# Relation counts of an adjacency layer: one-hots of the relations as weights instead of one-hots of the destinations

## The chip, the cores and the metric

The kernel runs on one core of a Trainium2 chip. The metric is the device time of one execution in microseconds, the median of three runs. The engines are TensorE (PE in the profile, its weight loads PEld), VectorE (DVE), ScalarE (ACT), GpSimd (POOL) and SyncE (SP), which issues most of the DMAs.

## What is computed

Four graph layers run one after the other on 3125 nodes of 128 features and 53125 edges (25000 drawn ones, their reverse, and a loop for each node), each followed by an addition of its input and a layer normalisation. Layer 0 is an attention layer, layer 1 sums the neighbours' rows, layer 2 weights them by an edge network, and layer 3 is a relational one:

```
rel_vec = rel_emb[edge_type]                        # 64 relations
msg = (x[src] + rel_vec) @ W_msg.T + b_msg
agg = segment_sum(msg, dst) / max(deg, 1)
out = x @ W_self.T + b_self + agg
```

Layer 3's sum of relation vectors into a node is the node's count of edges per relation times the table of 64 vectors. Neither those counts nor the adjacency matrix depends on features, and layer 1 needs the adjacency matrix as well. So both are built once, in layer 1.

## The kernel before, in words

Nodes are padded to 25 blocks of 128 (NB = 25). Edges are sorted into slots: a tile of 128 slots for each pair of a destination block and a source block. The phases follow one another: placing of the edges and the edge network (to some 200 us), layer 0 with gathers and scatters as one-hot matmuls (to 509 us), the **adjacency layer**, layer 1 (509 to 682 us), then layer 2 (gathers and scatters again) and layer 3, which reads the stored adjacency back.

The adjacency layer runs over 7 banks q of destination blocks (`even(q)`: four blocks in banks 0 to 3, three in banks 4 to 6) and, in each, over 25 source blocks b. That is 175 steps s = 25 q + b, and `even_width(q)` is 512 or 384 columns. For each step:

- VectorE makes the one-hots of the step's slots (`set_hots`, L1950) in one tile of `ring` (`ohs`, six buffers): for each slot the source node (128 values) and the relation (64 values). The block index d lies innermost, so that block d's one-hot has a stride of 4 elements. `ohx` holds the same for an extra tile of each bank, which is used at b = 0 and on the diagonal.
- The destination one-hots were stored in layer 0 (`hots_d`). SyncE loads them (L774, L778), contiguous for each block, into parts of `big` and `XT`, in chunks of five steps, four chunks ahead.
- TensorE's `build(s)` runs for each block d of the bank a matmul of the source one-hot (weights) with the destination one-hot (moving, 128 columns) into a bank that four steps take in turn (L2581; L2584 for the extra tile): the 128 x 128 block of the adjacency matrix. Then, for each block, it runs the relation counts (L2588; L2591 for the extra tile): **destination one-hot as weights, relation one-hot moving, 64 columns**. They add up over the whole bank q in PSUM bank 5 + q % 2, which a matmul with zeros clears first (L2560).
- ScalarE copies the adjacency block to fp32r (L1286); it or VectorE copies it to bytes (L1289, L1965), which SyncE stores for layer 3 (L804).
- TensorE's `apply1(s)` multiplies it by the features: two matmuls of 512 or 384 columns (L2611), adding up in PSUM bank 3 + q % 2; after a bank's last step the bank's own features are added (L2618), and VectorE copies the sums to `AG` (`sums_out1`, L1959, five steps into the next bank; `ag_ready`).

TensorE's program is written out by hand: two builds, then two applications, the builds two steps ahead. VectorE, ScalarE and SyncE keep to the same order of steps.

The counts of bank q stand in PSUM as destination x relation, while layer 3 needs relation x destination. So after bank q's last step ScalarE copies them to SBUF (`crelT`, L1295; semaphore `crelT_cp`). After the application of step 7 of bank q + 1 (after the last bank: at once), TensorE turns them (`rel_turned`, L2598), which needs `ag_ready`, since the transposes go to the bank of the sums (3 + q % 2). At b = 9 of bank q + 1 ScalarE copies the turned counts to `crel` (`rel_rows`, L1276; `crel_cp`) and SyncE stores them (L793).

At the end stands `dense` (L2642), the layer's weight matmul on seven groups of four blocks. Group i writes PSUM bank i, and VectorE adds each to the input (`relu_add`, L1994). Statistics, normalisation (ScalarE, L1227) and transposes follow in series.

Of the kernel before, what the change touches and what calls it, by code (L numbers as in the profile page):

```python
# [13 lines left out]
P = 128  # L14
# [14 lines left out]
NREL = 64  # L29
# [18 lines left out]
def gnn_kernel(nc, ins, out):  # L48
# [161 lines left out]
    with ctx:  # L210
# [3 lines left out]
        def sem(name):  # L214
            return ctx.enter_context(nc.semaphore(name))
# [80 lines left out]
        adjf = adjf_r[:, :].rearrange("p (r n) -> p r n", r=XBUF)  # L296
        identr = identr_r[:, :]
        crel = ring[:, 10240:10240 + 4 * 4 * P].bitcast(fp32).rearrange("p (r n) -> p r n", r=2)
        crelT = XT[:, HC:HC + 2 * CT].rearrange("p (r n) -> p r n", r=2)
        adj3 = ring[:, 0:3 * ACH * 2 * P].bitcast(u8).rearrange("p (r n) -> p r n", r=3)  # L300
        crel3 = ring[:, 7680:7680 + 4 * 4 * P].bitcast(fp32).rearrange("p (r n) -> p r n", r=2)

# [140 lines left out]
        def bank(i):  # L443
            return PS[:, 512 * i:512 * (i + 1)]
# [100 lines left out]
        applied = sem("applied")  # L545
        acc = sem("acc")
        crel_cp = sem("crel_cp")
        crel_tr = sem("crel_tr")
        crelT_cp = sem("crelT_cp")
        crel_io = [sem(f"crel_io{n}") for n in range(2)]  # L550
        ag_ready = sem("ag_ready")
        post = sem("post")
# [473 lines left out]
        def _(act):  # L1026
# [243 lines left out]

            def rel_rows(q):
                w = even_width(q)
                act.wait_ge(crel_tr, q + 1)
                if q >= 2:
                    act.wait_ge(crel_io[q % 2], 16 * (q // 2))
                C.copy(crel[0:NREL, q % 2, 0:w], bank(3 + q % 2)[0:NREL, 0:w]).then_inc(crel_cp, 1)  # L1276

            for q in range(BANKS):
                w = even_width(q)
                for b in range(NB):  # L1280
                    s = q * NB + b
                    act.wait_ge(adj_mm, s + 1)
                    if s >= XBUF:
                        act.wait_ge(applied, s - XBUF + 1)
                        dve_copied(act, s - XBUF)
                    C.copy(adjf[:, s % XBUF, 0:w], adj_bank(s)[:, 0:w]).then_inc(adjf_cp, 1)  # L1286
                    if not by_dve(s):
                        adj_free(act, s)
                        C.copy(adj_slot(s), adj_bank(s)[:, 0:w]).then_inc(adj_act, 1)  # L1289
                    if q == 0 and b % 2 == 0 and HBANK - 1 + b // 2 < BANKS:  # L1290
                        round_rows(1, HBANK - 1 + b // 2)
                    if q and b == 9:
                        rel_rows(q - 1)
                act.wait_ge(rel_mm, (q + 1) * NB)
                C.copy(crelT[:, q % 2, 0:w // 2], bank(5 + q % 2)[:, 0:w // 2]).then_inc(crelT_cp, 1)  # L1295
            rel_rows(BANKS - 1)

            normalise(2, X)
# [988 lines left out]
        def _(pe):  # L2287
# [234 lines left out]
            def sums(L):  # L2522
                kind, K, past = min(L, 1), gen_own(L), gen_past(L)
                if L == 1:
                    pe.wait_ge(ag_ready, BANKS)
                    pe.wait_ge(crelT_cp, BANKS)
                    pe.wait_ge(rc_cp, 1)
                    for b in range(NB):
                        o = T.transpose(PS[:, b * P:(b + 1) * P], X[:, b, :], ident[:, :])
                    o.then_inc(g_own, 1)  # L2530
                with pe.Fori(0, NCH) as c, pe.Fori(0, NB) as w:
                    m = pe.snap(c * (K + 2 * NB) + w * 2)
                    pe.wait_ge(g_step[kind], m + (past + K + 3))
                    if L == 0:
                        T.matmul(bank(0)[:, 0:VW], g_oh, g_vals, start=True, stop=True).then_inc(g_mm[kind], 1)
                    else:
                        T.matmul(bank(0)[:, 0:P], g_vals[:, 0:F], g_oh, start=True, stop=True).then_inc(g_mm[kind], 1)
                pe.wait_ge(g_step[kind], past + gen_total(L))
# [15 lines left out]
            def build(s):  # L2554
                q, b = s // NB, s % NB
                if b == 0:
                    pe.wait_ge(ohs_ready, q * JN + 2)
                    if q >= 2:
                        pe.wait_ge(crelT_cp, q - 1)
                    T.matmul(bank(5 + q % 2)[:, 0:even_width(q) // 2], zeros[0:1, 0:P], zeros[0:1, 0:even_width(q) // 2],  # L2560
                             start=True, stop=False, skip_group_check=True)
                pe.wait_ge(ohs_ready, q * JN + b + 2)
                if s == 3:
                    pe.wait_ge(rc_cp, 1)
                if s >= 4:
                    pe.wait_ge(adjf_cp, s - 3)
                    act_copied(pe, s - 4)
                c = q * NCK + b // ACH
                if b % ACH == 0:
                    hots_wait(pe, c)  # L2570
                both = even(q)

                def hots(buf, to, d):
                    return (buf[:, 0:OH1].rearrange("p (n b) -> p n b", b=4)[:, :, d], to[:, d, :],
                            buf[:, OH1:OH1 + CT].rearrange("p (n b) -> p n b", b=4)[:, :, d])

                usual = (ohs[:, s % SBUF, :], hots_in[c % HBUF][:, :, b % ACH, :])
                extra = (ohx[:, q % 2, :], hots_ex[:, q % 2, :, :])
                for d, blk in enumerate(both):
                    s1, d1, _ = hots(*usual, d)  # L2580
                    o = T.matmul(adj_bank(s)[:, d * P:(d + 1) * P], s1, d1, start=True, stop=blk != b)  # L2581
                    if blk == b:
                        s1, d1, _ = hots(*extra, d)
                        o = T.matmul(adj_bank(s)[:, d * P:(d + 1) * P], s1, d1, start=False, stop=True)  # L2584
                o.then_inc(adj_mm, 1)
                for d, blk in enumerate(both):
                    _, d1, r1 = hots(*usual, d)
                    o = T.matmul(bank(5 + q % 2)[:, d * NREL:(d + 1) * NREL], d1, r1, start=False, stop=False, skip_group_check=True)  # L2588
                    if b == 0:
                        _, d1, r1 = hots(*extra, d)  # L2590
                        o = T.matmul(bank(5 + q % 2)[:, d * NREL:(d + 1) * NREL], d1, r1, start=False, stop=False, skip_group_check=True)  # L2591
                o.then_inc(rel_mm, 1)

            def rel_turned(q):
                pe.wait_ge(crelT_cp, q + 1)
                pe.wait_ge(ag_ready, q + 1)
                for d in range(len(even(q))):
                    o = T.transpose(bank(3 + q % 2)[0:NREL, d * P:(d + 1) * P], crelT[:, q % 2, d * NREL:(d + 1) * NREL], ident[:, :])  # L2598
                o.then_inc(crel_tr, 1)

            def apply1(s):
                q, b = s // NB, s % NB
                w = even_width(q)
                if b == 0 and q >= 2:
                    pe.wait_ge(crel_cp, q - 1)
                if q == 0:
                    pe.wait_ge(xp_rest, b // 4 + 1)
                pe.wait_ge(adjf_cp, s + 1)
                to = bank(3 + q % 2)
                for part, xs in enumerate((XH, XL)):  # L2610
                    o = T.matmul(to[:, 0:w], xs[:, b, :], adjf[:, s % XBUF, 0:w], start=b == 0 and part == 0, stop=False, skip_group_check=True)  # L2611
                o.then_inc(applied, 1)
                if b == NB - 1:
                    if q == 0:
                        pe.wait_ge(identr_ready, 1)
                    for d, blk in enumerate(even(q)):
                        for xs in (XH, XL):
                            o = T.matmul(to[:, d * P:(d + 1) * P], xs[:, blk, :], identr, start=False, stop=False, skip_group_check=True)  # L2618
                    o.then_inc(acc, 1)
# [4 lines left out]
            for s in range(0, NS, 2):  # L2624
                for n in (s + 2, s + 3):
                    if n < NS:
                        build(n)
                for n in (s, s + 1):
                    if n < NS:
                        apply1(n)  # L2630
                        if n >= NB and n % NB == 7:
                            rel_turned(n // NB - 1)
            rel_turned(BANKS - 1)
            with pe.If(general == 1):
                sums(1)

# [16 lines left out]

            def sums1_wait(i):
                pe.wait_ge(ag_ready, (even_need(i) if i < 3 else BANKS))
                if i == 3:
                    pe.wait_ge(crel_cp, BANKS)
                if i >= 5:
                    pe.wait_ge(crelT_cp, BANKS)
                if i == 0:  # L2660
                    pe.wait_ge(rc_cp, 1)

            dense(post, sums1_wait, [(AG, W1[:, :])])
# [182 lines left out]
```

## Time and profile before

| | |
|---|---|
| median of 3 runs | 1089.4 us (1089.07 to 1090.24) |
| profiled execution | 1089.84 us, its span 1088.0 us |
| TensorE busy | 1002.6 us, 92% |
| VectorE busy | 861.1 us, 79% |
| ScalarE busy | 691.3 us, 64% |
| granted TensorE clock, mean | 0.971 |
| adjacency layer | 509 to 682 us of the span |

The profile is that of one execution. A line such as `L2588 PE MATMUL PS<-ring,big 128*128 128x64 bf16` is a group of instructions of one source line: engine, operation, tiles written and read, weights (partitions * columns) and moving operand (partitions x columns). A matmul's duration holds its latency, so several are in flight at a time; the distance of their starts is what the engine spends on one. In a timeline, neighbours of one line are merged into one row ("x4"), which gives the first start and the time to the last end.

### The profile page before, as it was taken

What the parts mean: (1) busy time and instruction counts of PE and PEld (TensorE: products, weight loads), DVE (VectorE), ACT (ScalarE), POOL (GpSimd) and SP (SyncE); (2) the same over time, 40 slices, a digit from 0 to 9 for tenths busy, and PEclk for the clock granted to TensorE, in tenths of its full rate; (3) what the DMA queues carried; (4) which work ended last, traced back from release to release, by engine and by line L of the source; (5) the groups of instructions that cost most, each with busy time, mean ns of one, the idle gap of its engine ahead of it and who ended that gap; (6) DMA issues with size and microseconds to landing.
All of it is one profiled execution on the core that took longest, in us unless ns stands there. A gap on an engine that the chain in (4) does not pass through costs nothing.

```text
span 1088.0 us, 27899 instructions
## 1 busy us (share of the span) xinstructions
PE 1002.6 (92%) x10463; PEld 874.7 (80%) x10463; DVE 861.1 (79%) x1934; ACT 691.3 (64%) x1489; POOL 218.2 (20%) x260
## 2 busy tenths in 40 slices
PE   3798979699999999995999999779999999989997
PEld 3343557599999999995788889669999999976775
DVE  6875999988998989987766677788787888766754
ACT  3467765454555555456888888577677776776554
POOL 4501340000000000000000000126666666610000
PEclk9899999899999999997999999889999999999998
DMA  6000020366767677752866564235444445334232
GB/s 159 1 2 1 4 68 3 121 207 225 238 215 225 222 238 227 204 175 72 292 195 193 172 201 141 82 104 140 138 136 129 131 131 139 109 112 124 69 99 82
DMA packets 86925, 150.38 MB, mean 138 GB/s; under 512 B 14524, under 2 KB 58375, under 8 KB 86557
## 3 DMA queue, kind: packets, MB, share of 16 engines
q1 hardware_dynamic: 65609, 116.01, 35.9%
q10 hardware_dynamic: 16122, 22.16, 5.7%
q0 software_dynamic: 5056, 10.36, 3.9%
q8 instruction: 88, 1.44, 0.5%
q14 instruction: 50, 0.40, 0.1%
HBM read 112.56 MB, written 35.94 MB: 136 GB/s over the span
## 4 chain that ended last, share of the span: by engine, by line
PE 81%; DVE 10%; ACT 4%; issue 3%; DMA 2%; POOL 0%; POOLq 0%; DVEq 0%; SPq 0%; ACTq 0%
PE PS L2500 14%; PE PS L2705 14%; PE PS L2488 11%; PE PS L2688 8%; PE PS L2611 7%; PE PS L2791 6%; PE PS L2581 3%; PE PS L2588 3%; PE PS L2326 2%; PE PS L2339 2%; DVE ring L1659 2%; DVE vo L1663 2%; PE PS L2403 2%; ACT X L1227 1%; PE PS L2357 1%
## 5 line engine op out<-in xcount | busy, mean ns | idle before, releaser
L1151 ACT CAST vo<-XT 128x768 f32<-128x768 bf16 (+1 forms) x218 | 180.3, 827 | 163.7 <-PE PS L2705 64.2
L984 POOL DMA_INDIRECT XT<-tab,ring x158 | 159.9, 1012 | 113.5 <-PE PS L2705 60.2
L2500 PE MATMUL PS<-vo 128*128 128x133 f32 x1300 | 175.9, 284 | 1.2 <-ACT vo L1151 1.2
L2500 PEld LDWEIGHTS PS<-vo 128*128 128x128 f32 x1300 | 157.2, 191 | 1.4 <-issue 1.4
L2488 PE MATMUL PS<-kp,ring 128*128 128x132 bf16 x1950 | 146.7, 221 | 3.2 <-DVE ring L1631 1.7
L2705 PE MATMUL PS<-vo 128*128 128x128 f32 x984 | 132.8, 279 | 0.0
L2488 PEld LDWEIGHTS PS<-kp,ring 128*128 128x128 bf16 x1950 | 125.6, 97 | 5.4 <-DVE ring L1631 1.8
L1641 DVE TENSOR_TENSOR XT<-iotab,XT 128x768 bf16<-128x768 bf16 (+1 forms) x218 | 120.0, 551 | 3.2 <-DMA hots_d<-XT 1.5
L2705 PEld LDWEIGHTS PS<-vo 128*128 128x128 f32 x984 | 118.9, 191 | 3.0 <-issue 2.4
L2490 PE MATMUL PS<-SDP,ring 128*128 128x12 bf16 x650 | 110.2, 170 | 0.0
L1286 ACT CAST adjf_r<-PS 128x512 fp32r<-128x512 f32 (+1 forms) x175 | 92.4, 550 | 25.4 <-PE PS L2581 23.6
L1631 DVE TENSOR_SCALAR ring<-ring,pcolm 128x1664 bf16<-128x1664 bf16 x146 | 91.2, 652 | 18.9 <-PE PS L2688 15.5
L1767 DVE TENSOR_TENSOR vo<-PS,vo 128x768 f32<-128x768 f32 (+1 forms) x109 | 103.2, 947 | 0.7 <-ACT vo L1201 0.5
L2107 DVE TENSOR_TENSOR vo<-PS,EWS 128x640 f32<-128x640 f32 (+2 forms) x109 | 82.3, 755 | 27.1 <-PE PS L2688 26.9
L2688 PE MATMUL PS<-kp,ring 128*128 128x128 bf16 x1476 | 99.9, 219 | 0.8 <-ACT big L1308 0.8
L965 POOL IOTA ring<- 128x650 int32 x1 | 0.8, 759 | 477.5 <-PE PS L2588 477.5
L2688 PEld LDWEIGHTS PS<-kp,ring 128*128 128x128 bf16 x1476 | 91.3, 98 | 2.3 <-ACT big L1308 1.0
L1950 DVE TENSOR_TENSOR ring<-IN,SLc 128x768 bf16<-128x768 bf16 x182 | 91.4, 550 | 0.0
L2791 PE MATMUL PS<-adjf_r,xh_r 128*128 128x512 f32 (+1 forms) x175 | 70.6, 404 | 7.2 <-DVE adjf_r L2255 3.4
L2611 PE MATMUL PS<-adjf_r,xh_r 128*128 128x512 f32 (+1 forms) x175 | 72.9, 417 | 0.0
L1103 ACT ACTIVATE kp<-PS 128x512 f32<-128x512 f32 x104 | 57.6, 608 | 23.0 <-PE PS L2326 22.1
L2611 PE MATMUL PS<-adjf_r,xl_r 128*128 128x512 f32 (+1 forms) x175 | 65.3, 373 | 0.0
(350 smaller groups left out, 2008.6 us busy)
## 6 DMA issues: line engine op xcount, KB each, us to landing
ring<-rows_d SPq DMA_DIRECT2D x146, 416.0 KB, 5.8
hots_d<-XT ACTq DMA_DIRECT2D x108, 192.0 KB, 4.7
big<-hots_d SPq DMA_DIRECT2D x10, 640.0 KB, 5.3
XT<-hots_d SPq DMA_DIRECT2D x10, 640.0 KB, 4.8
adj_d<-ring SPq DMA_DIRECT2D x20, 320.0 KB, 2.4
big<-hots_d SPq DMA_DIRECT2D x8, 480.0 KB, 4.4
adj_d<-ring SPq DMA_DIRECT2D x15, 240.0 KB, 2.1
ring<-adj_d SPq DMA_DIRECT2D x11, 320.0 KB, 3.0
```

Of the source, the lines that this page charges most:

```text
L984: G.indirect_dma_start(far_rows[:, f % FBUF, :], None, tab[2], bass.IndirectOffsetOnAxis(ap=far_row[:, t:t + 1], axis=0)).then_inc(far_in[ ...
L1151: C.copy(ohd[:, k % 3, 0:n, :], ohb[:, k % 3, 0:n, :]).then_inc(hots_wide, 1)
L1286: C.copy(adjf[:, s % XBUF, 0:w], adj_bank(s)[:, 0:w]).then_inc(adjf_cp, 1)
L1641: V.tensor_tensor(ohb[:, k % 3, 0:n, :].rearrange("p t (h d) -> p t h d", d=2), iotab[:, :].rearrange("p (h d) -> p h d", d=2).unsqueeze(1 ...
L1767: V.tensor_tensor(va[:, :, :, 0:F].rearrange("p a i (h f) -> p a i h f", h=H), gathered(k, 0, F).rearrange("p a i (h f) -> p a i h f", h=H ...
L2488: T.matmul(PS[:, to:to + ROW0], ohT[:, 0, h % OBUF, l * P:(l + 1) * P], KP[:, source(t), part, :], start=part == 0, stop=part == 2)
L2490: T.matmul(PS[:, to + ROW0:to + ROW0 + 3 * H], ohT[:, 1, h % OBUF, l * P:(l + 1) * P], SDP[:, t // JN, :, :].rearrange("p t h -> p (t h)") ...
L2500: T.matmul(bank(6 + b % 2)[:, 0:VW], ohd[:, k % 3, i, :], vals[:, k % 3, i, :], start=j == 0, stop=j == JN - 1).then_inc(scattered, 1)
L2611: o = T.matmul(to[:, 0:w], xs[:, b, :], adjf[:, s % XBUF, 0:w], start=b == 0 and part == 0, stop=False, skip_group_check=True)
L2688: o = T.matmul(PS[:, to:to + F], ohT[:, 0, h % OBUF, l * P:(l + 1) * P], XP[:, source(t), part, :], start=part == 0, stop=part == 2)
L2705: T.matmul(bank(6 + q % 2)[:, (b % 4) * P:(b % 4 + 1) * P], rows_of(k, i, t), ohd[:, k % 3, i, :], start=j == 0, stop=j == JN - 1).then_in ...
L2791: o = T.matmul(to[:, 0:w], xs[:, b, :], adjf[:, s % XBUF, 0:w], start=b == 0 and part == 0, stop=False, skip_group_check=True)
```

## The change

The operands of the relation matmuls are exchanged: the relation one-hot (64 columns, at a stride of 4 elements) becomes the weights, the destination one-hot (128 columns, contiguous) moves. The result is relation x destination in 64 partitions and 128 columns for each block, up to a whole PSUM bank. The zeroing matmul is as wide. The transposes, `crelT`, its copies and the two semaphores go. ScalarE copies the counts straight from bank 5 + q % 2 to `crel`, at b = 2 of the next bank instead of b = 9; TensorE's waits follow: the clearing of a counts bank waits for `crel_cp` two banks back, the first application in a bank of sums for `ag_ready` two banks back, and the weight matmuls at the end wait for all ScalarE's byte copies before group 0 and for `crel_cp` only before group 5.

```diff
--- before.py
+++ after.py
@@ -296,7 +296,6 @@
         adjf = adjf_r[:, :].rearrange("p (r n) -> p r n", r=XBUF)
         identr = identr_r[:, :]
         crel = ring[:, 10240:10240 + 4 * 4 * P].bitcast(fp32).rearrange("p (r n) -> p r n", r=2)
-        crelT = XT[:, HC:HC + 2 * CT].rearrange("p (r n) -> p r n", r=2)
         adj3 = ring[:, 0:3 * ACH * 2 * P].bitcast(u8).rearrange("p (r n) -> p r n", r=3)
         crel3 = ring[:, 7680:7680 + 4 * 4 * P].bitcast(fp32).rearrange("p (r n) -> p r n", r=2)
 
@@ -545,8 +544,6 @@
         applied = sem("applied")
         acc = sem("acc")
         crel_cp = sem("crel_cp")
-        crel_tr = sem("crel_tr")
-        crelT_cp = sem("crelT_cp")
         crel_io = [sem(f"crel_io{n}") for n in range(2)]
         ag_ready = sem("ag_ready")
         post = sem("post")
@@ -1270,10 +1267,10 @@
 
             def rel_rows(q):
                 w = even_width(q)
-                act.wait_ge(crel_tr, q + 1)
+                act.wait_ge(rel_mm, (q + 1) * NB)
                 if q >= 2:
                     act.wait_ge(crel_io[q % 2], 16 * (q // 2))
-                C.copy(crel[0:NREL, q % 2, 0:w], bank(3 + q % 2)[0:NREL, 0:w]).then_inc(crel_cp, 1)
+                C.copy(crel[0:NREL, q % 2, 0:w], bank(5 + q % 2)[0:NREL, 0:w]).then_inc(crel_cp, 1)
 
             for q in range(BANKS):
                 w = even_width(q)
@@ -1289,10 +1286,8 @@
                         C.copy(adj_slot(s), adj_bank(s)[:, 0:w]).then_inc(adj_act, 1)
                     if q == 0 and b % 2 == 0 and HBANK - 1 + b // 2 < BANKS:
                         round_rows(1, HBANK - 1 + b // 2)
-                    if q and b == 9:
+                    if q and b == 2:
                         rel_rows(q - 1)
-                act.wait_ge(rel_mm, (q + 1) * NB)
-                C.copy(crelT[:, q % 2, 0:w // 2], bank(5 + q % 2)[:, 0:w // 2]).then_inc(crelT_cp, 1)
             rel_rows(BANKS - 1)
 
             normalise(2, X)
@@ -2523,7 +2518,7 @@
                 kind, K, past = min(L, 1), gen_own(L), gen_past(L)
                 if L == 1:
                     pe.wait_ge(ag_ready, BANKS)
-                    pe.wait_ge(crelT_cp, BANKS)
+                    pe.wait_ge(crel_cp, BANKS)
                     pe.wait_ge(rc_cp, 1)
                     for b in range(NB):
                         o = T.transpose(PS[:, b * P:(b + 1) * P], X[:, b, :], ident[:, :])
@@ -2556,8 +2551,8 @@
                 if b == 0:
                     pe.wait_ge(ohs_ready, q * JN + 2)
                     if q >= 2:
-                        pe.wait_ge(crelT_cp, q - 1)
-                    T.matmul(bank(5 + q % 2)[:, 0:even_width(q) // 2], zeros[0:1, 0:P], zeros[0:1, 0:even_width(q) // 2],
+                        pe.wait_ge(crel_cp, q - 1)
+                    T.matmul(bank(5 + q % 2)[0:NREL, 0:even_width(q)], zeros[0:1, 0:NREL], zeros[0:1, 0:even_width(q)],
                              start=True, stop=False, skip_group_check=True)
                 pe.wait_ge(ohs_ready, q * JN + b + 2)
                 if s == 3:
@@ -2585,24 +2580,17 @@
                 o.then_inc(adj_mm, 1)
                 for d, blk in enumerate(both):
                     _, d1, r1 = hots(*usual, d)
-                    o = T.matmul(bank(5 + q % 2)[:, d * NREL:(d + 1) * NREL], d1, r1, start=False, stop=False, skip_group_check=True)
+                    o = T.matmul(bank(5 + q % 2)[0:NREL, d * P:(d + 1) * P], r1, d1, start=False, stop=False, skip_group_check=True)
                     if b == 0:
                         _, d1, r1 = hots(*extra, d)
-                        o = T.matmul(bank(5 + q % 2)[:, d * NREL:(d + 1) * NREL], d1, r1, start=False, stop=False, skip_group_check=True)
+                        o = T.matmul(bank(5 + q % 2)[0:NREL, d * P:(d + 1) * P], r1, d1, start=False, stop=False, skip_group_check=True)
                 o.then_inc(rel_mm, 1)
-
-            def rel_turned(q):
-                pe.wait_ge(crelT_cp, q + 1)
-                pe.wait_ge(ag_ready, q + 1)
-                for d in range(len(even(q))):
-                    o = T.transpose(bank(3 + q % 2)[0:NREL, d * P:(d + 1) * P], crelT[:, q % 2, d * NREL:(d + 1) * NREL], ident[:, :])
-                o.then_inc(crel_tr, 1)
 
             def apply1(s):
                 q, b = s // NB, s % NB
                 w = even_width(q)
                 if b == 0 and q >= 2:
-                    pe.wait_ge(crel_cp, q - 1)
+                    pe.wait_ge(ag_ready, q - 1)
                 if q == 0:
                     pe.wait_ge(xp_rest, b // 4 + 1)
                 pe.wait_ge(adjf_cp, s + 1)
@@ -2628,9 +2616,6 @@
                 for n in (s, s + 1):
                     if n < NS:
                         apply1(n)
-                        if n >= NB and n % NB == 7:
-                            rel_turned(n // NB - 1)
-            rel_turned(BANKS - 1)
             with pe.If(general == 1):
                 sums(1)
 
@@ -2653,11 +2638,10 @@
 
             def sums1_wait(i):
                 pe.wait_ge(ag_ready, (even_need(i) if i < 3 else BANKS))
-                if i == 3:
+                if i == 5:
                     pe.wait_ge(crel_cp, BANKS)
-                if i >= 5:
-                    pe.wait_ge(crelT_cp, BANKS)
                 if i == 0:
+                    act_copied(pe, NS - 1)
                     pe.wait_ge(rc_cp, 1)
 
             dense(post, sums1_wait, [(AG, W1[:, :])])
```

## Rows read from the trace of the kernel before

**Rows 1.** The page, busy time and share of the span of TensorE.

```profile
PE 1002.6 (92%) x10463; PEld 874.7 (80%) x10463; DVE 861.1 (79%) x1934; ACT 691.3 (64%) x1489; POOL 218.2 (20%) x260
```

**Rows 2.** Busy us by stretch: length, PE, PEld, DVE, ACT, POOL, clock, DMA share, GB/s.

```profile
549.00:576.00 27.00, 27.00 (x281) 22.21 (x280) 17.43 (x38) 22.14 (x44) 0.00 (x0) 1.00 0.64 197
```

**Rows 3.** Timeline of a pair of four-block steps: start us, us, engine line, tiles.

```profile
581.43 0.42 PE L2581 MATMUL PS<-big,ring 128*128 128x128 bf16 x4
...
581.69 0.40 PE L2588 MATMUL PS<-ring,big 128*128 128x64 bf16 x4
...
581.91 0.41 PE L2581 MATMUL PS<-big,ring 128*128 128x128 bf16 x4
...
582.15 0.40 PE L2588 MATMUL PS<-ring,big 128*128 128x64 bf16 x4
...
582.36 0.47 PE L2611 MATMUL PS<-adjf_r,xh_r 128*128 128x512 f32 x1
...
583.38 0.41 PE L2581 MATMUL PS<-big,ring 128*128 128x128 bf16 x4
```

**Rows 4.** Timeline early in the first bank, with the wait for a one-hot.

```profile
524.90 0.26 PEld L2581 LDWEIGHTS PS<-XT,ring 128*128 128x128 bf16 x4 [0.58 <-DVE ring L1950]
```

**Rows 5.** Timeline of TensorE, three-block steps: a plain pair, then one with transposes.

```profile
645.45 0.36 PE L2581 MATMUL PS<-XT,ring 128*128 128x128 bf16 x3
...
646.93 0.36 PE L2581 MATMUL PS<-XT,ring 128*128 128x128 bf16 x3
647.13 0.34 PE L2588 MATMUL PS<-ring,XT 128*128 128x64 bf16 x3
647.29 0.35 PE L2581 MATMUL PS<-XT,ring 128*128 128x128 bf16 x3
...
648.74 0.36 PE L2581 MATMUL PS<-XT,ring 128*128 128x128 bf16 x3
```

**Rows 6.** Timeline of the four-block pair that holds the transposes.

```profile
549.89 0.41 PE L2581 MATMUL PS<-XT,ring 128*128 128x128 bf16 x4
...
552.27 0.41 PE L2581 MATMUL PS<-XT,ring 128*128 128x128 bf16 x4
```

**Rows 7.** Timeline of the layer's end.

```profile
679.39 0.48 ACT L1289 CAST ring<-PS 128x384 uint8<-128x384 f32 x1
...
680.61 0.27 PE L2618 MATMUL PS<-identr_r,xl_r 128*128 128x128 f32 x1
680.92 0.56 DVE L1959 COPY big<-PS 128x384 f32<-128x384 f32 x1 [1.87 <-PE PS L2618]
...
682.02 5.82 PE L2642 MATMUL PS<-W,big 128*128 128x128 f32 x50
...
683.19 0.69 DVE L1994 SCALAR_TENSOR_TENSOR big<-PS,X 128x512 f32<-128x512 f32 x1 [1.71 <-PE PS L2642]
```

**Rows 8.** Single lines, ns min/median/max; the last two, of the page: busy us, mean ns.

```profile
L2581 PEld LDWEIGHTS PS<-big,ring x320: 111/115/152, 510.1 to 674.4; 128*128 128x128 bf16 x160
...
L2588 PEld LDWEIGHTS PS<-ring,big x320: 96/98/152, 510.5 to 674.6; 128*128 128x128 bf16 x160
L2588 PE MATMUL PS<-ring,big x320: 217/239/261, 510.6 to 674.6; 128*128 128x64 bf16 x160
...
L2318 PEld LDWEIGHTS PS<-identb,big x104: 123/124/209, 35.5 to 139.5; 128*99 128x99 bf16 x104
...
L2705 PEld LDWEIGHTS PS<-vo 128*128 128x128 f32 x984 | 118.9, 191 | 3.0 <-issue 2.4
...
L2688 PE MATMUL PS<-kp,ring 128*128 128x128 bf16 x1476 | 99.9, 219 | 0.8 <-ACT big L1308 0.8
```

**Rows 9.** Timelines elsewhere: plain matmuls, ones behind 99-column loads, fp32 weight loads.

```profile
819.82 0.94 PE L2688 MATMUL PS<-kp,ring 128*128 128x128 bf16 x14
...
59.86 0.39 PE L2318 MATMUL PS<-identb,big 128*99 128x128 bf16 x4
...
820.54 1.08 PEld L2705 LDWEIGHTS PS<-vo 128*128 128x128 f32 x9
```

## The prediction

> **What bounds the kernel now.** I read the page's busy shares, then a table of busy time by stretch over the adjacency layer, then the timeline of single steps there, steps with four destination blocks and with three, and last the end of the layer. TensorE is busy for 92% of the span [rows 1], so an edit in its stream may count. In the adjacency layer TensorE is busy for the whole of a stretch of 27.00 us, with ScalarE at 22.14 and VectorE at 17.43 [rows 2]. ScalarE and VectorE thus have a sixth or more to spare, and TensorE sets the pace. The timeline says the same: a pair of steps runs from 581.43 to 583.38 us, 1.95 us, and consecutive TensorE rows follow without a gap [rows 3]. Only early in the first bank does TensorE wait for one-hots; the last time is at 524.90 [rows 4], some 14 steps in, so I take 14 of the 100 four-block steps (banks 0 to 3) as covered by waits, and 86 plus the 75 three-block steps (banks 4 to 6) as TensorE bound. That is 86 x 4 + 75 x 3 = 569 relation matmuls that count.
>
> The rows start by start give the price of a matmul, since lasting 219 or 239 ns is latency and the spacing is what is paid. In the pair of rows 3 the adjacency matmuls (L2581) take 0.26 + 0.24 us for eight, 0.0625 each; the relation matmuls (L2588) take 0.22 + 0.21 us for eight, 0.054 each. In a three-block step they take 0.20 and 0.16 us for three, 0.067 and 0.053 [rows 5].
>
> **The change, part by part.**
>
> *Turns inside the layer, removed.* A pair of four-block steps that holds the four transposes runs from 549.89 to 552.27, 2.38 us [rows 6] against 1.95: 0.43. A three-block pair with its three runs from 646.93 to 648.74, 1.81 us, and the plain pair before it from 645.45, 1.48 us [rows 5]: 0.33. Turns of banks 0 to 3 and 4 to 5: 4 x 0.43 + 2 x 0.33 = **-2.4 us**.
>
> *The tail.* Today the last applications start at 680.61, VectorE copies the sums from 680.92 for 0.56 us, only then do the last transposes run, and the dense matmuls (L2642) begin at 682.02; VectorE takes their first bank at 683.19, 1.17 us later [rows 7]. After the change the first dense bank needs only the sums of bank 0, and ScalarE's last byte copy, which starts at 679.39 and lasts 0.48 us [rows 7], so it can begin at some 680.72. VectorE would take it at 681.9, after its own copy (until 681.48). **-1.3 us**. Behind it stands a serial chain (VectorE's additions and statistics, ScalarE's scaled rows), so I expect it kept. Relation bank 6 is needed only at the dense matmuls' bank 5, microseconds later; nothing waits there. Late next is VectorE's own sequence.
>
> *The zeroing matmul, wider.* It goes from 256 to 512 columns (192 to 384). At the 0.0555 us that 128 bf16 columns take [rows 9] (worked out below), 256 more columns are 0.111 us and 192 are 0.083. Six banks after the first: 3 x 0.111 + 3 x 0.083 = **+0.6 us**; the lower bound is nothing, if the wait for a one-hot covers it. In bank 0 it is covered.
>
> *The copies.* ScalarE loses seven copies of counts and keeps the other seven, moved from the tenth step of a bank to the third. With a sixth to spare these are nothing; the cover is TensorE's pace, and a copy of 0.6 us put into the wrong place costs at most a part of that, seven times. ScalarE's idle share is spread over the steps, so I take 0. SyncE's store of the counts waits for the copy, which now comes earlier, and the block loads queued behind it are four ahead: 0. TensorE's new waits (the count copy two banks back in place of the turned copy; the sums two banks back) are for things done most of a bank earlier: 0.
>
> *The relation matmul itself.* This is the open term. Before: weights 128 columns, contiguous, moving 64 columns at a stride of 4 elements. After: weights 64 columns at that stride, moving 128 contiguous. The moving side first. The 64 strided columns last 239 ns, more than the 219 ns of 128 contiguous ones, and are spaced 0.054 us, not half of a 128-column matmul [rows 3, 8]. Fourteen plain 128-column matmuls elsewhere take 0.94 us: (0.94 - 0.219) / 13 = 0.0555 each [rows 9]. So doubling the columns costs 0.0015 each, 569 x 0.0015 = +0.9. On this the Trainium skill disagrees: TensorE: Matmul & The Clock Gate, section Back-to-back issue gap, has N / 2.4 + 2.5 ns at the full clock, so about 29 ns for 64 columns and 56 for 128; SBUF — State Buffer, section Door 1 (the passage on 16-byte cachelines), lets bf16 be strided by up to 8 elements for free, so it would not excuse the strided read either. By these the edit would add 27 ns to each, some +15 us. This case's trace disagrees: 0.054 us for 64 columns; the measurement decides.
>
> Then the weight side. A 128-column strided load lasts 115 ns against 98 contiguous, and a contiguous one of 99 columns 124 ns [rows 8]: fewer columns aren't quicker, narrower loads seem to run in a slower form. Four matmuls behind such 99-column loads are still spaced (0.39 - 0.219) / 3 = 0.057 [rows 9]. Loads of 128 fp32 columns follow each other every (1.08 - 0.191) / 8 = 0.111 us [rows 8, 9], so 64 columns at that rate need 0.056. Both rows point to 0.057, and I take that: 569 x 0.003 = **+1.7 us**. Bounds: 0.0555 from below (+0.9), from above 0.0625, what matmuls behind strided loads cost now (+4.8), and farther off the fp32 0.111 (+32). The Trainium skill, TensorE: Matmul & The Clock Gate, section Weight-path perf modes, says that the fast weight load is on only with 128 non-fp32 columns, so this edit would lose it; with the P / 1.2 ns of its section on LDWEIGHTS a plain load is 53 ns, an estimate, just under the moving side; the 124 ns of the 99-column load bear out that a narrow load loses something. By that estimate alone the sum would keep +0.9.
>
> **Sum**: -2.4 - 1.3 + 0.6 + 1.7 = **-1.4 us**. The profiled execution took 1089.84 us, 1.84 around a span of 1088.0; it would be 1088.4. The median of the three runs is 0.44 below that execution, so I forecast 1088.0.
>
> **The rivals.**
>
> *A, the whole group tightens.* The adjacency matmuls' 0.0625 may come from the neighbouring strided moving reads, not from their own strided loads. With all at 0.0555 a four-block step falls by 0.465 - 0.444 = 0.021, a three-block step by 0.36 - 0.333 = 0.027: 86 x 0.021 + 75 x 0.027 = -3.8 in place of +1.7, in all -6.9: 1082.5. For: the rows of plain matmuls. Against: their own loads are longer, 115 against 98 ns, and the relation group beside them is already at 0.054.
>
> *B, slower: the narrow strided load sticks out.* At L2588 each matmul waits for its load. At 0.0625 the sum is +1.7, 1091.1, still no measurable change; at 0.070, 569 x 0.016 = 9.1 less 3.1, +6.0: 1095.4. It decides from 0.0634 on (569 x 0.0094 = 5.3, less 3.1, is +2.2). For: 124 ns for 99 columns, with a stride on top here. Against: 64 columns are fewer, and that load was hidden.
>
> *C, the load at the full fp32 price*, 0.111: +32 - 3.1, 1118. Against: it would need 64 columns to be as slow as 128.
>
> *D, the turns were covered (no change).* With TensorE quicker at the turns, VectorE's one-hots or the ScalarE copy moved to the third step come late, and only the tail is gained: -1.3 + 2.3 = +1.0, 1090.4. Against: the idle shares of rows 2.
>
> *E, columns decide.* Were 64 moving columns today at half the price of 128, 0.0278, with the rest of their 0.054 cover for something else that stays, the group would grow by 569 x 0.0278 = 15.8, less 3.1: 1102. The 0.054 speaks against it almost fully. It is what the Trainium skill's section Back-to-back issue gap, named above, would have.
>
> **How the numbers follow.** Forecast 0.50 (its own range, relation spacing 0.0555 to 0.060: 1087.1 to 1089.7), A 0.12, B 0.22, D 0.08, C 0.04, E 0.02, the rest smaller things. Within 0.2% means 2.2 us of 1089.4, about what a measurement of this kernel can tell. Faster: A and the third of the forecast at its lower bound, with turns worth a little more than I took (the last 0.1 us to the bound): 0.32. Slower: over half of B, C and E: 0.19. Same: 0.49. The range is 1085.0 to 1094.0; outside lie A, the far part of B, C and E.
>
> **What would show it.** No L2598; pairs of bank turns like their neighbours (1.95); dense matmuls from some 1.3 us after the last application. A pair of four-block steps 0.02 us longer than now; 0.07 longer is B, 0.04 shorter is A. The relation load's duration: 111 to 145 ns. If ScalarE or VectorE appears as the releaser of L2581 around the third step of a bank, D is right. The forecast is wrong if the relation group of four isn't within 0.22 to 0.24 us.

## The result and the profile after

The changed kernel takes 1133.8 us (median of 4 runs, 1132.09 to 1135.8) where the kernel before takes 1089.82 beside it: a ratio of 1.0409, 95% interval 1.0396 to 1.0421. That is 44 us slower, far outside the range. The page's busy shares and its clock row answer to [rows 1]:

```profile
PE 1051.6 (93%) x10438; PEld 895.6 (79%) x10438; DVE 861.7 (76%) x1934; ACT 694.3 (61%) x1482; POOL 217.6 (19%) x260
...
PEclk9898999899999999998999999979999999999998
```

TensorE is busier by 49 us, the clock is granted as before. The stretch of [rows 2], same columns:

```profile
549.00:576.00 27.00, 27.00 (x220) 20.03 (x218) 14.57 (x32) 18.09 (x36) 0.00 (x0) 1.00 0.52 159
```

TensorE is still busy throughout, ScalarE is down from 22.14 to 18.09 us and VectorE from 17.43 to 14.57. ScalarE waits more for TensorE's adjacency blocks, from the table of who waited for whom in the layer (us in total, times, longest):

```profile
ACT adjf_r L1283 <- PE PS L2576: 63.1, 90, 2.0
```

It was 23.2 us before. A pair of four-block steps, to be held against [rows 3]; L2576 is the adjacency matmul (before: L2581), L2583 the relation matmul (before: L2588), L2599 the application (before: L2611):

```profile
601.10 0.41 PE L2576 MATMUL PS<-big,ring 128*128 128x128 bf16 x4
601.44 0.46 PE L2583 MATMUL PS<-big,ring 128*64 128x128 bf16 x4
601.83 0.41 PE L2576 MATMUL PS<-big,ring 128*128 128x128 bf16 x4
602.18 0.46 PE L2583 MATMUL PS<-big,ring 128*64 128x128 bf16 x4
602.56 0.50 PE L2599 MATMUL PS<-adjf_r,xh_r 128*128 128x512 f32 x1
...
603.61 0.41 PE L2576 MATMUL PS<-big,ring 128*128 128x128 bf16 x4
```

The pair takes 2.51 us instead of 1.95. A group "holds" TensorE from its first start to the first start of the next group. Four adjacency matmuls now hold 0.34 or 0.35 us (before 0.26 and 0.24), four relation matmuls 0.39 and 0.38 (0.22 and 0.21). A three-block pair has grown by the same amount, although it has fewer matmuls, from 1.48 us [rows 5] to 2.05:

```profile
702.80 0.36 PE L2576 MATMUL PS<-XT,ring 128*128 128x128 bf16 x3
...
704.85 0.36 PE L2576 MATMUL PS<-XT,ring 128*128 128x128 bf16 x3
```

So the loss is a price for each passage from one group to the other and not for each matmul. One passage closely, first the kernel before, adjacency to relation (weight loads are PEld):

```profile
677.56 0.22 PE L2581 MATMUL PS<-XT,ring 128*128 128x128 bf16 x1
677.56 0.21 PEld L2588 LDWEIGHTS PS<-ring,XT 128*128 128x128 bf16 x3
677.62 0.34 PE L2588 MATMUL PS<-ring,XT 128*128 128x64 bf16 x3
```

The load for the relation matmul starts at 677.56, with the adjacency matmul before it, and the two matmuls start 0.06 us apart. After:

```profile
724.07 0.22 PE L2576 MATMUL PS<-XT,ring 128*128 128x128 bf16 x1
724.22 0.26 PEld L2583 LDWEIGHTS PS<-XT,ring 128*64 128x64 bf16 x3
724.22 0.40 PE L2583 MATMUL PS<-XT,ring 128*64 128x128 bf16 x3
```

The load no longer starts with the matmul before it at 724.07 but 0.15 us later, and the relation matmul starts together with it and not sooner. The load itself, ns min/median/max:

```profile
L2583 PEld LDWEIGHTS PS<-big,ring x320: 134/145/178, 512.6 to 720.1; 128*64 128x64 bf16 x160
```

That is 145 ns in the middle, the upper end of the 111 to 145 ns that the prediction gave as its sign.

### The profile page after: what moved, and what is told of

Same layout as the page of the kernel before. It is cut to its first block, busy times and chain, and to the rows that moved or that the text cites. A ratio compares the mean times of both kernels' runs of the same rounds, so it can differ in the third digit from the quotient of the medians.

```text
span 1134.0 us, 27833 instructions
## 1 busy us (share of the span) xinstructions
PE 1051.6 (93%) x10438; PEld 895.6 (79%) x10438; DVE 861.7 (76%) x1934; ACT 694.3 (61%) x1482; POOL 217.6 (19%) x260
## 4 chain that ended last, share of the span: by engine, by line
PE 83%; DVE 9%; ACT 4%; issue 2%; DMA 1%; POOL 0%; POOLq 0%; DVEq 0%; SPq 0%; ACTq 0%
PE PS L2495 14%; PE PS L2689 13%; PE PS L2483 11%; PE PS L2599 8%; PE PS L2672 7%; PE PS L2583 6%; PE PS L2775 5%; PE PS L2576 4%; PE PS L2321 2%; PE PS L2334 2%; PE PS L2398 2%; DVE vo L1658 1%; DVE ring L1654 1%; ACT X L1224 1%; PE PS L2352 1%
## 5 line engine op out<-in xcount | busy, mean ns | idle before, releaser
L1283 ACT CAST adjf_r<-PS 128x512 fp32r<-128x512 f32 (+1 forms) x175 | 95.3, 545 | 70.2 <-PE PS L2576 63.1
L1960 DVE CAST ring<-adjf_r 128x512 uint8<-128x512 f32 (+1 forms) x70 | 27.9, 398 | 81.7 <-ACT adjf_r L1283 81.7
L2599 PE MATMUL PS<-adjf_r,xh_r 128*128 128x512 f32 (+1 forms) x175 | 74.5, 426 | 0.0
L1100 ACT ACTIVATE kp<-PS 128x512 f32<-128x512 f32 x104 | 57.6, 608 | 23.2 <-PE PS L2321 22.3
```

## The experiments

Two theories stand against each other. **S, the switch**: passing from weights of 128 columns to weights of 64, or back, stops the early load of the next weights. **N, the narrow operand**: each 64-column load, or its output in 64 partitions, costs by itself. Each kernel below ran beside the kernel before on one chip.

**Weights 128 columns wide.** The last 64 source one-hots, which lie beside the relation one-hots at the same stride, come along as weights, so the counts come out in partitions 64 to 127. The zeroing matmul is 128 wide too (in the diffs, "..." marks what is left out).

```diff
-buf[:, OH1:OH1 + CT].rearrange("p (n b) -> p n b", b=4)[:, :, d]
+buf[:, CT:OH1 + CT].rearrange("p (n b) -> p n b", b=4)[:, :, d]
...
-o = T.matmul(bank(5 + q % 2)[0:NREL, d * P:(d + 1) * P], r1, d1, ...
+o = T.matmul(bank(5 + q % 2)[:, d * P:(d + 1) * P], r1, d1, ...
...
-C.copy(crel[0:NREL, q % 2, 0:w], bank(5 + q % 2)[0:NREL, 0:w])
+C.copy(crel[0:NREL, q % 2, 0:w], bank(5 + q % 2)[P - NREL:P, 0:w])
```

> The changed kernel, but the relation matmul's weights are 128 columns wide: the last 64 source one-hots and the 64 relation one-hots, which lie beside each other at the same stride; the counts come out in PSUM partitions 64 to 127 and are copied from there. Theory S (switch): going from weights of 128 columns to weights of 64 and back stops the early loading of the next weights; each of the two changes in a step costs some 0.1 us or a bit more, 0.25 us in a step with the slower first matmuls after them. Nothing switches here, so the pair of steps falls from about 2.4 to 1.95 to 2.0 us and the kernel takes 1086 to 1093 us. Theory N (the narrow operand itself, its load or its output in 64 partitions, is slow) expects the same, as nothing is narrow. If the moving operand of 128 columns were what costs, it would stay at about 1134.

1083.95 us, ratio 0.9955 (95% interval 0.9938 to 0.9971): not only is the loss gone, the kernel is faster than the kernel before.

```profile
599.77 0.42 PE L2576 MATMUL PS<-big,ring 128*128 128x128 bf16 x4
600.03 0.39 PE L2583 MATMUL PS<-big,ring 128*128 128x128 bf16 x4
600.25 0.39 PE L2576 MATMUL PS<-big,ring 128*128 128x128 bf16 x4
600.47 0.39 PE L2583 MATMUL PS<-big,ring 128*128 128x128 bf16 x4
600.67 0.48 PE L2599 MATMUL PS<-adjf_r,xh_r 128*128 128x512 f32 x1
...
601.68 0.41 PE L2576 MATMUL PS<-big,ring 128*128 128x128 bf16 x4
```

The pair takes 1.91 us, the relation groups hold 0.22 and 0.20 us, the adjacency groups 0.26 and 0.22. 128 moving columns instead of 64 cost nothing. S and N both allow this; the next ones part them.

**As many narrow loads, half the switches.**

```diff
-                o.then_inc(adj_mm, 1)
-                for d, blk in enumerate(both):
+                o.then_inc(adj_mm, 1)
+                return q, b, both, hots, usual, extra
+
+            def relate(q, b, both, hots, usual, extra):
+                for d, blk in enumerate(both):
...
+                for made in [build(n) for n in steps if n < NS]:
+                    relate(*made)
```

> The changed kernel with its 64-column weights, but TensorE runs the adjacency matmuls of both steps of a pair first and then the relation matmuls of both: two changes of weight width for a pair instead of four, with as many narrow loads. Theory S: half of the cost goes, about 0.25 us a pair, 1110 to 1115 us. Theory N: every narrow load costs, no change, 1131 to 1136 us.

1111.06 us, 1.0200 (1.0180 to 1.0221), within what S expected.

```profile
591.57 0.50 PE L2603 MATMUL PS<-adjf_r,xh_r 128*128 128x512 f32 x1
...
592.61 0.64 PE L2572 MATMUL PS<-big,ring 128*128 128x128 bf16 x8
593.17 0.70 PE L2587 MATMUL PS<-big,ring 128*64 128x128 bf16 x8
593.81 0.50 PE L2603 MATMUL PS<-adjf_r,xh_r 128*128 128x512 f32 x1
```

The pair, from application to application, takes 2.24 us, 0.27 less than in the changed kernel, with the same matmuls in another order. Eight relation matmuls in one group hold 0.64 us, where two groups of four held 0.77. N is out as the main cause: it expected no change.

**96 columns.** As the wide one, with 96 weight columns; the relation counts that layer 3 uses are not the right rows.

```diff
+buf[:, OH1 - 128:OH1 + CT].rearrange("p (n b) -> p n b", b=4)[:, :, d]
...
+o = T.matmul(bank(5 + q % 2)[0:96, d * P:(d + 1) * P], r1, d1, ...
```

> As e1_wide, but with 96 columns of weights (32 source and 64 relation one-hots), and the copy takes the first 64 rows of what comes out, so the relation counts that layer 3 uses are not the right ones. Theory S in the form that the array's division counts (64 columns are half of it, 96 need the whole): no stop at the changes, weight loads some 0.01 to 0.03 us longer than those of 128, 1088 to 1100 us. Theory S in the form that any change between a 128-column load and another one stops: 1125 to 1140 us. Theory N in the form of the slower kind of load: 1120 to 1150 us, at e1_wide's time plus the longer loads.

1103.38 us, 1.0130 (1.0109 to 1.0150), above the range of S in the form of the array's division, and below the others.

```profile
591.99 0.52 PE L2583 MATMUL PS<-big,ring 128*96 128x128 bf16 x4
592.34 0.39 PE L2576 MATMUL PS<-big,ring 128*128 128x128 bf16 x4
```

The relation group holds 0.35 us for its four matmuls. The load's line:

```profile
L2583 PEld LDWEIGHTS PS<-big,ring x320: 163/186/205, 510.6 to 690.2; 128*96 128x96 bf16 x160
```

There is no stop at the passages (a first adjacency group of the same timeline runs from 591.74 to 591.99, 0.25 us, as before), but the load of 96 strided columns lasts 186 ns and spaces the matmuls 0.0875 us apart. So a narrower load does cost by itself, and the expectation had put that too low: 0.13 us for each of the 86 bound four-block steps and 0.10 for each of the 75 three-block ones make up the 19 us over the wide kernel. It is another effect than the stop. Widths between 64 and 96 were not tried.

**The old order of operands, narrow and contiguous.** The counts of 64 of each block's 128 destinations are left out.

```diff
-o = T.matmul(bank(5 + q % 2)[:, d * NREL:(d + 1) * NREL], d1, r1, ...
+o = T.matmul(bank(5 + q % 2)[0:64, d * NREL:(d + 1) * NREL], d1[:, 0:64], r1, ...
```

> The kernel before, operands in the old order, but only the first 64 of the 128 destination one-hots are the weights of the relation matmul (contiguous), so the counts of the other 64 destinations of a block are left out. Theory S: four stops in a pair as in the changed kernel, 1125 to 1140 us, although neither stride, nor the moving operand, nor anything else of the change is here. If the stride of the narrow load is needed for the stop, it stays at 1088 to 1092 us.

1128.75 us, 1.0363 (1.0342 to 1.0383).

```profile
592.88 0.42 PE L2581 MATMUL PS<-big,ring 128*128 128x128 bf16 x4
593.23 0.41 PE L2588 MATMUL PS<-ring,big 128*64 128x64 bf16 x4
593.57 0.42 PE L2581 MATMUL PS<-big,ring 128*128 128x128 bf16 x4
```

```profile
L2588 PEld LDWEIGHTS PS<-ring,big x320: 106/109/159, 511.2 to 712.3; 128*64 128x64 bf16 x160
```

Nothing of the change is in this kernel but the width of 64, the loads are contiguous and short (109 ns), and the adjacency group holds 0.35 us, the relation group 0.34. The stop needs neither stride nor exchange.

**Everything of the change but the exchange.** The zeroing matmul stays 512 columns wide, with 128-column weights. The counts are not turned, so layer 3 uses wrong ones.

```diff
-o = T.matmul(bank(5 + q % 2)[0:NREL, d * P:(d + 1) * P], r1, d1, ...
+o = T.matmul(bank(5 + q % 2)[:, d * NREL:(d + 1) * NREL], d1, r1, ...
```

> Everything of the change but the exchange of the operands: no transposes, no copies for them, the later waits, the wider zeroing; the relation matmul runs as before (128-column weights, 64 columns moving). The counts are not turned, so layer 3 uses wrong ones. The prediction priced these parts at -2.4 - 1.3 + 0.6 = -3.1 us: 1085.5 to 1086.5 where the kernel before has 1089. If the switch of weight widths is the whole cause of the loss, this keeps the gain in full. A rival in which the freed time is taken up by waits elsewhere (the prediction's D) expects -0.5 to -1.3 us.

1086.0 us, 0.9967 (0.9954 to 0.9981), -3.6 us with an interval of -5.0 to -2.1. The expected gain is all there; the pair takes 1.94 us as before:

```profile
600.64 0.41 PE L2576 MATMUL PS<-big,ring 128*128 128x128 bf16 x4
...
602.58 0.41 PE L2576 MATMUL PS<-big,ring 128*128 128x128 bf16 x4
```

**The wide kernel again, without its zeroing, without its stride.** Three kernels beside the last.

> e1_wide once more, beside the next kernel on one chip: 0.9955 of the kernel before, 1083 to 1086 us. Against e6_no_turns it shows what the exchange alone does when the weights stay 128 wide: -1 to -3 us if matmuls behind strided loads come as close as any others once the strided moving operand is gone, +1 to +5 us if the strided load is dearer than the strided moving operand.

1084.48 us, 0.9944 (0.9931 to 0.9958), -6.1 us. Against the last kernel the exchange gives -2.5 us by the ratios and -1.5 by the medians; the two intervals overlap a little, so its size is rough, but no loss is seen.

Without the zeroing matmul, the bank's first relation matmul starts the sum:

```diff
-                    T.matmul(bank(5 + q % 2)[:, 0:even_width(q)], zeros[0:1, 0:P], zeros[0:1, 0:even_width(q)],
-                             start=True, stop=False, skip_group_check=True)
...
-... r1, d1, start=False,
+... r1, d1, start=b == 0 and d == 0,
```

> e1_wide without the zeroing matmul of each bank: the bank's first relation matmul starts the sum instead. The zeroing matmul's weights have 1 row, so it is a change of the array's division too, and the timeline shows 0.25 to 0.4 us for it in each bank. Theory S: both its stream and two stops go, six times 0.3 us or so, 1.2 to 2.4 us below e7_wide_again. If a change of rows doesn't stop the array, only the stream of 512 columns goes, six times 0.15 to 0.2 us: 0.6 to 1.2 us.

1081.89 us, 0.9929 (0.9915 to 0.9943), -7.7 us and the fastest of all. Against the wide kernel 1.6 us by the ratios, 2.6 by the medians, with overlapping intervals. The timelines are clearer. With the zeroing, at the start of the second bank, then without:

```profile
537.38 0.41 PE L2576 MATMUL PS<-big,ring 128*128 128x128 bf16 x4
...
537.95 0.39 PE L2555 MATMUL PS<-zeros 1*128 1x512 bf16 x1
538.26 0.41 PE L2576 MATMUL PS<-big,ring 128*128 128x128 bf16 x4
```

```profile
538.50 0.41 PE L2574 MATMUL PS<-big,ring 128*128 128x128 bf16 x4
...
538.97 0.39 PE L2574 MATMUL PS<-big,ring 128*128 128x128 bf16 x4
```

A step with the zeroing takes 0.88 us, one without 0.47: 0.41 in each bank, 2.5 us for the six that count. At 0.0555 for 128 columns its 512 columns stream for 0.22, so the rest, 0.19, looks like a stop on either side. A change of weight rows, 128 to 1, thus seems to stop the array as well. In the kernel before, with 256 columns, a zeroing took 0.31 us (591.14 to 591.93, less the 0.48 of a step): the wider one costs 0.10 more, as priced.

With contiguous weights, which are other elements of the same tile, so adjacency and counts are wrong:

```diff
-return (buf[:, 0:OH1].rearrange("p (n b) -> p n b", b=4)[:, :, d], to[:, d, :],
-        buf[:, CT:OH1 + CT].rearrange("p (n b) -> p n b", b=4)[:, :, d])
+return (buf[:, d * P:(d + 1) * P], to[:, d, :],
+        buf[:, CT + d * P:CT + (d + 1) * P])
```

> e1_wide, but the weights of the adjacency and of the relation matmuls are read contiguous (other elements of the same tile, so adjacency and counts are wrong). It measures what the stride of 4 elements still costs: if the load of 113 ns instead of 98 is hidden, 0 to 1 us less than e7_wide_again; if it sets the spacing (0.0625 against 0.0555 us), 3 to 8 us less, as far as ScalarE at 83% leaves room.

1083.61 us, 0.9943 (0.9927 to 0.9958), the same as with the stride; the pair takes 1.90 us against 1.91:

```profile
600.11 0.40 PE L2576 MATMUL PS<-big,ring 128*128 128x128 bf16 x4
...
602.01 0.40 PE L2576 MATMUL PS<-big,ring 128*128 128x128 bf16 x4
```

The strided load of 128 columns is hidden behind the matmuls.

**More switches.** Same matmuls as the changed kernel, relation behind adjacency for each block.

```diff
                 for d, blk in enumerate(both):
...
-                o.then_inc(adj_mm, 1)
-                for d, blk in enumerate(both):
+                    if d == len(both) - 1:
+                        o.then_inc(adj_mm, 1)
```

> The changed kernel, with the relation matmul of each destination block right behind that block's adjacency matmul. The same matmuls, but 8 changes of weight width in a four-block step instead of 2 and 6 in a three-block step. Theory S: e2_grouped, with 1 change a step, took 22.7 us less than the changed kernel, so a change costs some 0.13 us; 6 x 100 + 4 x 75 = 900 more changes are +115 us: 1220 to 1270 us. A theory in which the narrow loads cost: no change, 1134 us.

1388.37 us, 1.2739 (1.2700 to 1.2777): 254 us over the changed kernel, more than twice what S expected.

```profile
700.21 0.29 PE L2576 MATMUL PS<-big,ring 128*128 128x128 bf16 x1
700.44 0.32 PE L2583 MATMUL PS<-big,ring 128*64 128x128 bf16 x1
700.69 0.30 PE L2576 MATMUL PS<-big,ring 128*128 128x128 bf16 x1
```

Each matmul now takes 0.23 to 0.25 us instead of 0.06. The stretch (length, PE, PEld, DVE, ACT, POOL, clock, DMA share, GB/s) shows why it is more:

```profile
600.00:700.00 100.00, 100.00 (x356) 56.11 (x355) 23.59 (x50) 29.57 (x54) 0.00 (x0) 0.50 0.22 68
```

The granted clock is 0.50, the 1.2 GHz level, though the table calls TensorE busy for all 100 us. The kernel before, the changed kernel and this one all enter the layer at 0.50 (509 to 518 us), after TensorE was busy for 0.4 us or less of the 6 before. The changed kernel has 0.99 from 520 to 549 us and 1.00 behind; this one stays at 0.50 to the layer's end at some 980 us. S priced the stops at the full clock; here they come with every matmul, and the applications between them run at the lower level too. This run therefore bears out the direction and not the price of a stop.

**All narrow.**

```diff
+                        for h in range(2):
+                            o = T.matmul(adj_bank(s)[64 * h:64 * h + 64, d * P:(d + 1) * P], s1[:, 64 * h:64 * h + 64], d1,
+                                         start=part is usual, stop=blk != b or part is extra)
```

> The changed kernel with the adjacency matmul cut in two halves of 64 weight columns, for PSUM partitions 0 to 63 and 64 to 127: within the builds of a pair no load has another width than its neighbour, and four matmuls a step are added. Theory S: two stops in a pair remain (at the applications) instead of four; if the halves run one after the other at 0.060 us each, +0.24 us a step for them and -0.25 us a pair, 1145 to 1160 us; if the halves run side by side, 1100 to 1120 us. If narrow loads were what costs 0.06 us or more each, 1180 us or more.

1112.03 us, 1.0203 (1.0169 to 1.0238), what S expected with halves side by side.

```profile
601.44 0.46 PE L2578 MATMUL PS<-XT,ring 128*64 128x128 bf16 x8
601.74 0.41 PE L2583 MATMUL PS<-XT,ring 128*64 128x128 bf16 x4
602.08 0.40 PE L2555 MATMUL PS<-zeros 1*64 1x512 bf16 x1
```

Eight half-width adjacency matmuls hold 0.30 us up to the first relation matmul, 0.0375 each: the halves overlap, and no stop stands between the narrow groups. With four matmuls more in each four-block step and every build load narrow it is 22 us faster than the changed kernel. Narrow loads among narrow loads are cheap. The last line shows a change of rows alone, since the zeroing's weights are 64 wide like their neighbours: it starts 0.34 us after the relation group, where four spacings of 0.06 would be 0.24.

**A narrow group that does not stop.** The kernel before has groups of 64-column weights too, the fp32 transposes (L2598), in the pair of [rows 6]:

```profile
551.13 0.39 PE L2611 MATMUL PS<-adjf_r,xl_r 128*128 128x512 f32 x1
551.13 0.56 PEld L2598 LDWEIGHTS PS<-ident,XT 128*64 128x64 f32 x4
551.36 0.60 PE L2598 MATMUL PS<-ident,XT 128*64 128x128 f32 x4
551.71 0.48 PE L2611 MATMUL PS<-adjf_r,xh_r 128*128 128x512 f32 x1
```

Their first load starts with the application matmul before it at 551.13, the first transpose 0.23 us later, as one application matmul after another does, and the four hold 0.35 us up to the next application. So no stop is seen on either side, and 64 columns are not enough by themselves. Not every fp32 group is exempt, it seems: before the 32-column fp32 matmuls of the edge network the load stands idle for nothing that the profile shows.

```profile
92.92 0.16 PEld L2339 LDWEIGHTS PS<-kp,Zb 128*32 128x32 f32 x8 [0.42 <-issue]
```

That points to the transposing and not to the type as what spares L2598, but no run here parts the two.

## Why the prediction was wrong

**The step that failed** is the relation matmul's weight side. It took the 99-column loads and the fp32 loads of [rows 8, 9] as a price per matmul, 0.057, and multiplied by 569. The spacing inside the group was about right: the later matmuls of a group start 0.06 us apart. What it left out, and so put at nothing, is what happens between a group of one width and a group of another. The 99-column load could not show it: it belongs to a transpose, and the 64-column transposes above don't stop either. The run with 96 columns has no stops, while those with 64 among 128 have them, with the operands in either order and with or without a stride. So what counts isn't "less than 128". That it is a division of the array, which 64 columns get and 96 don't, is an inference; the overlapping halves of the all-narrow kernel speak for it. The Trainium skill has this: TensorEngine Tiling (Array Packing), section Key Properties, "Mode switching requires drain". It names no price, and the prediction did not draw on it, since nothing in the code asks for tiling; in these bf16 matmuls a 64-column weight operand is enough. This case's traces agree for them, but not for the fp32 transposes above, and they give the price: some 0.10 us where a narrow group begins, some 0.17 over a narrow group until the next wide load works, and 0.03 at the first application, 0.57 a pair. By the trace and the model of the steps, 161 bound steps x 0.285 = 46 us, less the 3.1 of the other parts: 43, measured 44.

The prediction also had the rule of the Trainium skill, TensorE: Matmul & The Clock Gate, section Weight-path perf modes, that the fast weight load is on only with 128 non-fp32 columns. These traces show a size for it: a load of 96 strided columns lasts 186 ns, of 64 strided 145 and of 64 contiguous 109, against 113 for 128 strided and 98 for 128 contiguous.

**The other steps.** *What bounds the kernel*: right; a loss in TensorE's stream came through in full. *Turns, tail and zeroing*, -3.1: measured -3.6 in the kernel without the exchange. In the tail VectorE took the first dense bank 2.58 us after the start of the last L2618 [rows 7]; now, with L2606 and L2627 in their place:

```profile
727.70 0.27 PE L2606 MATMUL PS<-identr_r,xl_r 128*128 128x128 f32 x1
...
727.81 3.45 PE L2627 MATMUL PS<-W,big 128*128 128x128 f32 x29
...
728.95 0.69 DVE L1989 SCALAR_TENSOR_TENSOR big<-PS,X 128x512 f32<-128x512 f32 x1 [0.39 <-PE PS L2627]
```

1.25 us after, so 1.33 gained for the 1.3 predicted. *Copies, waits, SyncE*: priced at nothing, and the -3.6 leaves no room for a loss there. *Moving side*: right, and a little better than priced: with the weights 128 wide the relation group of four holds 0.20 to 0.22 us. The columns rule (rival E), which would have had 1102 us, is refuted by the 1084 of the kernel with 128-column weights.

**The rivals.** A (the group tightens) was half right, in the wide kernel: the second adjacency group fell from 0.24 to 0.22 us. It needed the width to stay. B and C had the right side and the wrong mechanism: C's 1118 is the nearest number by chance, since the matmuls of a group start 0.06 us apart and not 0.111. D didn't occur: the kernel without the exchange keeps the whole gain. The sign for "wrong" that the prediction gave, a relation group of four outside 0.22 to 0.24 us, is what the trace shows: 0.39. Its other sign, a load of 111 to 145 ns, held and gave no warning.

## What to carry to other kernels

Before exchanging the operands of a matmul, look at the widths of the weights beside it in TensorE's stream, and count the changes of width, not the matmuls: a group of 64-column bf16 weights among 128-column ones costs more than a quarter of a microsecond here, whether it has three, four or eight matmuls. If the narrow operand has neighbours in memory, take them along to 128 columns and read the wanted partitions of the result; that turned 44 us lost into 5 to 6 us won. A row of the trace proves a price only for the transitions it contains: ask what stood before and behind it, and whether it was a transpose.

## What the runs showed that was not expected

- 64 and 96 bf16 weight columns differ in kind: 96 has no stop but a load of 186 ns and matmuls 0.0875 us apart; 64 has a stop and a load of 109 to 145 ns.
- Transposes with 64-column fp32 weights have no stop.
- 64 moving bf16 columns at a stride of 4 elements (0.052 to 0.055 us in a group) take as long as 128 contiguous ones.
- Halves of 64 weight columns in different output partitions overlap: 0.0375 us a matmul.
- With a stop at every matmul the granted clock stayed at 0.50 for the whole layer while TensorE counted as busy; 900 more switches took 254 us, the lower clock included.
- A zeroing matmul with 1-row weights cost 0.41 us where its columns stream for 0.22 (an estimate from 0.0555 for 128).
